# The last stage of an attention and experts kernel: one copy moved, a chunk's end split, doubled expert weights, the last chunk's end in halves

## What is computed

```python
    x = L0_attn_x
    x = x + _layernorm(_L0_attn_ref(_layernorm(x, axis=-1), ...), axis=-1)
    x = x + _layernorm(_L0_ffn_ref(_layernorm(x, axis=-1), ...), axis=-1)
...
        scores0 = x[:, 0, :] @ Wr + br
        _, idx = jax.lax.top_k(scores0, k)
        W1g, b1g = (W1[idx], b1[idx])
        W2g, b2g = (W2[idx], b2[idx])
        h = jnp.einsum('bsd,bkde->bkse', x, W1g) + b1g[:, :, None, :]
        h = jax.nn.gelu(h, approximate=False)
        o = jnp.einsum('bkse,bkef->bksf', h, W2g) + b2g[:, :, None, :]
        return jnp.sum(o, axis=1) / k
```

## Time and profile before

| | us |
|---|---|
| median of 3 runs (2047.66 to 2054.5) | 2049.87 |
| the profiled execution's own time | 2049.51 |
| its span, first to last instruction | 2047.8 |
| PE, DVE, ACT, POOL busy in the span | 1976.5, 1791.3, 1363.0, 305.4 |
| last stage, from its first matrix product at 1690.6 | 357.2 |

### The profile page before, as it was taken

How to read it: one execution, slowest core, us unless ns; L and a number is a source line. 1 busy time by engine, 2 the same in 40 slices (tenths; PEclk the granted TensorE clock), 3 DMA queues, 4 the chain that set the end, 5 groups by cost and what they waited for, 6 DMA issues and landing times.

```text
span 2047.8 us, 39736 instructions
## 1 busy us (share of the span) xinstructions
PE 1976.5 (97%) x15772; PEld 869.5 (42%) x15772; DVE 1791.3 (87%) x3564; ACT 1363.0 (67%) x1653; POOL 305.4 (15%) x373
## 2 busy tenths in 40 slices
PE   9999999999999999999999999999999996999996
PEld 6655333333333333333333333333333324667664
DVE  6876999999999999989999999999899917898883
ACT  5766757777777777777777777777777781333332
POOL 4333101011010101011010101111010104322000
PEclk9999999999999999999999999999999997999999
DMA  5877515050322304041423505051332034454320
GB/s 171 259 230 202 111 37 101 7 92 22 79 50 49 74 23 91 8 90 27 77 45 51 91 8 90 7 92 34 67 58 41 17 109 113 116 138 112 91 67 31
DMA packets 144907, 162.44 MB, mean 79 GB/s; under 512 B 52946, under 2 KB 118610, under 8 KB 144722
## 3 DMA queue, kind: packets, MB, share of 16 engines
q1 hardware_dynamic: 137554, 147.26, 31.2%
q0 software_dynamic: 7168, 12.64, 2.8%
HBM read 99.77 MB, written 59.77 MB: 78 GB/s over the span
## 4 chain that ended last, share of the span: by engine, by line
PE 81%; DVE 11%; ACT 4%; issue 2%; DMA 1%; SPq 1%; POOL 0%; ACTq 0%; POOLq 0%; DVEq 0%
PE b_psO L1121 25%; PE b_psS L1104 25%; PE b_ring L615 13%; PE a_psQK L906 6%; DVE b_pmax L631 4%; PE c_psH L1501 3%; PE a_psV L918 3%; PE c_psO L1514 3%; ACT b_prob L1068 2%; PE b_ring L613 1%; PE c_psA L1471 1%; DVE c_ln_x_stats L81 1%; DVE c_attn L105 1%; DVE c_ln_f_stats L81 1%; PE a_psT L881 1%
## 5 line engine op out<-in xcount | busy, mean ns | idle before, releaser
L631 DVE TENSOR_REDUCE b_pmax<-b_ring 128x1 f32<-128x512 f32 (+4 forms) x2284 | 1336.7, 648 | 75.1 <-PE b_ring L615 59.2
L1068 ACT ACTIVATE b_prob<-b_psS 128x1024 f32<-128x1024 f32 (+3 forms) x1280 | 1085.2, 895 | 367.3 <-PE b_psS L1104 362.6
L1104 PE MATMUL b_psS<-g_qT,g_kT 64*128 64x512 bf16 (+6 forms) x5120 | 833.2, 347 | 10.1 <-ACT b_prob L1068 7.2
L615 PE MATMUL b_ring<-g_kT,g_qT 64*128 64x512 bf16 (+2 forms) x2500 | 714.5, 348 | 2.9 <-DVE b_pmax L631 1.5
L1121 PE MATMUL b_psO<-b_prob,g_v 128*32 128x512 f32 (+3 forms) x5120 | 595.0, 540 | 0.3
L1104 PEld LDWEIGHTS b_psS<-g_qT,g_kT 64*128 64x128 bf16 (+1 forms) x5120 | 295.4, 94 | 460.6 <-ACT b_prob L1068 343.4
L1039 POOL TENSOR_SCALAR_AFFINE_SELECT b_prob<-b_prob 128x512 f32<-128x512 f32 x256 | 162.7, 636 | 1315.8 <-ACT b_prob L1068 1315.5
L615 PEld LDWEIGHTS b_ring<-g_kT,g_qT 64*128 64x128 bf16 x2500 | 221.2, 94 | 234.2 <-DVE b_pmax L631 162.4
L613 PE MATMUL b_ring<-later,query_of 64*128 64x128 bf16 x988 | 191.9, 219 | 3.0 <-DVE b_pmax L631 2.4
L1121 PEld LDWEIGHTS b_psO<-b_prob,g_v 128*32 128x32 f32 x5120 | 103.4, 108 | 172.1 <-issue 131.9
L1501 PE MATMUL c_psH<-c_yT,c_w1e 128*128 128x512 f32 x256 | 119.4, 613 | 22.0 <-ACT c_hT L1426 21.7
(11 more groups left out here) (119 smaller groups left out, 1060.5 us busy)
## 6 DMA issues: line engine op xcount, KB each, us to landing
qk_parts<-a_parts SPq DMA_DIRECT2D x64, 384.0 KB, 4.5
g_qT<-qk_parts SPq DMA_DIRECT2D x184, 128.0 KB, 3.9
g_kT<-qk_parts SPq DMA_DIRECT2D x184, 128.0 KB, 5.1
out_sums<-b_outT SPq DMA_DIRECT2D x64, 256.0 KB, 2.4
v_ones<-a_v SPq DMA_DIRECT2D x16, 544.0 KB, 5.8
g_v<-v_ones SPq DMA_DIRECT2D x32, 272.0 KB, 5.3
a_x<-in_L_attn_x SPq DMA_DIRECT2D x16, 512.0 KB, 5.2
c_x<-in_L_attn_x SPq DMA_DIRECT2D x16, 512.0 KB, 7.3
```

The lines of the kernel that those rows point to most:

```text
L615: ins_ = self.nc.tensor.matmul(to, groups.qT[own, g, h // 2, 0, t * P:(t + 1) * P], groups.kT[own, g, h // 2, 0, pc * CH:pc * CH + w], sta ...
L631: self.nc.vector.tensor_reduce(pmax[:, c % 2].rearrange("p (h t) n -> p h t n", t=TT)[:, heads[0]:heads[-1] + 1:2, qt, pc], bank[:, 0:k * ...
L1068: nc.scalar.activation(prob[:, j % PBUF, 2 * s:2 * s + 2, off:CH], psS[:, 2 * s:2 * s + 2, off:CH], ACT.Exp).then_inc(exp_done, 1)
L1104: ins_ = nc.tensor.matmul(psS[:, 2 * s + p, off:CH], kT[own, g, s, ab, kt * P:(kt + 1) * P], qT[own, g, s, ab, c * CH + off:(c + 1) * CH], ...
```

## The change

Four edits, all in `stage_c` (and the number of tiles becomes a parameter of `LayerNorm`).

1. ACT's order: copy_y(n+2) comes ahead of root_ffn(n). From step 13 on the order is another one: step 13 is gelu(13), copy_y(15), gelu(14), root_ffn(13); step 14 is gelu(15), root_ffn(14); step 15 is root_ffn(15).
2. DVE's order: `experts_end` is cut after the variance. The rest (normalise, add, release the store) is a new function `experts_out`, and take_projection(n+4) stands between the two.
3. Two sets of expert weights and biases, chosen by the parity of the sequence. SP's two waits ahead of overwriting now look one sequence further back and fall away for the first two sequences.
4. The last chunk's end is done in two halves of two tiles, each with its own small layer norm (`ln_last`): `outer` raises `o_done` after tile 1 and after tile 3, DVE takes half 0 through to its output and then half 1, and SP stores each half with its own DMA.

In the diff stand, in this order, the waits of `load_experts` and the last stores on SP, the cut of `experts_end` with the two new functions on DVE, DVE's order and ACT's order:

```diff
-                if not (isinstance(b, int) and b == 0):
-                    sp.wait_ge(gelu_done, b * NC * 2 * KD + 2)
+                if b > 1:
+                    sp.wait_ge(gelu_done, (b - 1) * NC * 2 * KD + 2)
...
-                sp.wait_ge(o_read, b * NC + 1)
+                if b > 1:
+                    sp.wait_ge(o_read, (b - 1) * NC + 1)
...
+                        for h, t in enumerate(HALVES):
+                            sp.wait_ge(out_done, n + 1 + h)
+                            sp.dma_start(out_t[n, :, t], out_sb[:, c % 2, t]).then_inc(stored[c % 2], 16)
...
                 ln_f.variance(chain, ffn, var_f)
+            def experts_out(b, c, n):
+
+                p = c % 2
+                chain = Chain(v, chain_f, n * LN_MARKS + LN_MARKS - 1)
                 v.wait_ge(std_f, n + 1)
                 ln_f.normalise(chain, ffn, ffn).then_inc(norm_f, 1)
                 v.wait_ge(norm_f, n + 1)

                 v.wait_ge(stored[p], 16 + (b * 2 + c // 2) * 16)
                 nc.vector.tensor_tensor(out_sb[:, p], x1[:, c], ffn[:, :, :], ALU.add).then_inc(out_done, 1)
+
+            def last_end():
+
+                v.wait_ge(out_done, LAST)
+                v.wait_ge(stored[LAST % 2], 16 + (B * NC // 2 - 1) * 16)
+                for h, t in enumerate(HALVES):
+                    ln, chain = ln_last[h], Chain(v, chain_l[h], 0)
+                    v.wait_ge(o_done, LAST + 1 + h)
+                    chain.mark(nc.vector.scalar_tensor_tensor(
+                        out=ffn[:, t], in0=psO[:, t], scalar=0.5,
+                        in1=b2mean[:, :].unsqueeze(1).to_broadcast([P, TT // 2, D]), op0=ALU.mult, op1=ALU.add))
+                    chain.wait()
+                    ln.variance(chain, ffn[:, t], var_f)
+                    v.wait_ge(std_f, LAST + 1 + h)
+                    chain.mark(ln.normalise(chain, ffn[:, t], ffn[:, t]))
+                    chain.wait()
+                    nc.vector.tensor_tensor(out_sb[:, LAST % 2, t], x1[:, NC - 1, t], ffn[:, t], ALU.add
+                                            ).then_inc(out_done, 1)
...
                 for k, part in ((2, normalise_x1), (1, route), (3, add_attention), (0, experts_end),
-                                (4, take_projection), (2, route)):
+                                (4, take_projection), (0, experts_out), (2, route)):
...
-                order = ((0, gelu), (3, root_attn), (3, root_x1), (0, root_ffn), (2, copy_y))
+                n = b * NC + c
+                order = ((0, gelu), (3, root_attn), (3, root_x1), (2, copy_y), (0, root_ffn))
+                if n >= UNLED - 1:
+                    order = ((0, gelu),) * (n < UNLED) + ((2, copy_y), (1, gelu), (0, root_ffn))
```

More of the change, by code:

```diff
@@ L103, in normalise @@
         chain.wait()
-        for t in range(TT):
+        for t in range(self.tiles):
             last = v.tensor_scalar(dst[:, t], src[:, t], self.mean[:, t:t + 1], self.rstd[:, t:t + 1],
@@ L1188, in stage_c @@
         ln_f = LayerNorm(nc, sb, "c_ln_f")
+        ln_last = [LayerNorm(nc, sb, f"c_ln_l{h}", tiles=TT // 2) for h in range(2)]
         psT = pb("c_psT", [P, KD, CH], F32)
@@ L1222, in stage_c @@
         stored = [sem(f"c_stored{p}") for p in range(2)]
+        chain_l = [sem(f"c_chain_l{h}") for h in range(2)]
+        LAST = B * NC - 1
+        UNLED = LAST - 1
+        HALVES = [slice(0, TT // 2), slice(TT // 2, TT)]
         W_LOADS = 4
@@ L1289, in _ @@
             for p in range(2):
-                sp.wait_ge(stored[p], 16 + 16 * B * NC // 2)
+                sp.wait_ge(stored[p], 16 + 16 * (B * NC // 2 + p))
         @block.gpsimd
@@ L1402, in step @@
                             route(to_route(b, c))
+                    elif which and part in (experts_end, experts_out) and which[2] == LAST:
+                        if part is experts_end:
+                            last_end()
                     elif which:
```

64 lines of the change are left out of this document (35 added, 29 removed).

## The result

| | before | changed |
|---|---|---|
| median of four runs, us | 2052.18 (2047.66 to 2055.05) | 2034.54 (2033.25 to 2038.79) |
| the profiled execution, and its span | 2049.51, 2047.8 | 2038.79, 2037.1 |

What follows compares the result with a forecast made beforehand. PE was taken to set the pace, so its waits can be won: 2.7 (step 1) + 6.8 (middle) + 2.7 (step 13) + 2.84 + 2.81 + 0.7 = 18.55 us, from 2049.87 to 2031.4 us; range 2026.5 to 2036.5 (0.89).

Steps and rivals of the forecast that it cites:

- The tail on ACT: Steps 14 and 15: GELUs ahead of roots and table loads remove stalls of 2.57 and 2.55, gaining 2.84 and 2.81 us.
- the last end in halves: End of the last step: the split gives 0.4 us on DVE and the smaller second store 0.3 us.
- The middle steps: Nine steps from hidden(3): 5.1 us of smaller stalls, 0.5 of restarts, 1.2 of weight waits, 6.8 us in all.
- It shows only where DVE runs late, and I count it as 0: Split of the chunk's end: DVE's gain per step, some tenths of a us from a shorter root wait, counted as 0.
- DVE can follow at 18.1: Middle: steps 2, 5, 10 and 11 had no stall at 0.4 us lag, so DVE keeps up with 18.1 us steps.
- Two sets of experts: Outer in two steps: w2's DMAs go out some 2 us earlier, so the whole 1.2 us wait for weights goes.
- Step 1: Stall shrinks from 3.77 to 2.76 us and the eight products behind it take 3.7 us; 2.7 us gained.
- Step 13: Stall shrinks from 3.74 to 2.73 us and the products behind it run at the higher clock; 2.7 us gained.
- the lower clock stays: Rival, steps 1 and 13: one or both stalls of 2.75 us still cost 1.7; 2033.1 or 2034.8 us, chance 0.16.
- I take 0, since 2.75 is 0.2 from the stalls without it and 1.0 from those with it: Steps 1 and 13: clock loss behind each shortened stall, bounded by 0 and 1.7 us, is taken as 0.
- the signs of being wrong: Products of 5.4 us behind 2.75 stalls; POOL's product beside normalise_x1 and again the projection's; DVE waiting for `psO` at the end.
- the slower rival: Middle: POOL's product holds DVE twice a step, each stall 2.9 us, 21.3 us a step; 2052 us, chance 0.03.

Runs made afterwards that it cites:

- e5: Changed kernel with the last chunk's end in one piece (one layer norm, one store); median 2035.5 us.
- e4: Changed kernel with ACT's order in the tail as in all other steps (copy ahead of the root, then the GELUs); median 2036.5 us.
- e2: Changed kernel with the chunk's end undivided, experts_out ahead of take_projection; median 2040.02 us.
- e8: Changed kernel with POOL's product cut to 2 of 1024 columns from chunk 4 on, so results are wrong; 2031.0 us in a single run.
- e11: Changed kernel with POOL's product moved to DVE from chunk 4 on, two chunks earlier than needed, ahead of the attention's sum; median 2030.78 us.
- e1: Changed kernel with the copy behind the root again in all steps but the tail's; median 2038.06 us.
- e6: Kernel before with only the copy moved ahead of the root in every step; ratio 0.9993 (0.9972 to 1.0013) to the kernel before, median 2049.3 us.
- e3: Changed kernel with one set of experts' weights and SP's waits as before; median 2036.2 us.
- e7: Changed kernel with the average of the experts' last biases done ahead of the attention's sum on DVE; median 2032.5 us.
- e13: e11 with the tail's order one step earlier and without ACT's own wait for expert weights; median 2027.88 us, ratio 0.9879 to the kernel before.

## Why the prediction was right, and where it was not

- **The tail on ACT and the last end in halves** (2.84, 2.81 and 0.7 us): right in size and mechanism. Step 14 and the last stretch came out at 13.77 and 23.51 us as summed, and DVE's half 1 followed half 0 with no wait for PE. e5 bears out the 0.7; e4 shows both stalls come back (1.68 and 2.55 us).
- **The middle steps** (6.8 us): the sum was right (6.2 and 7.3 us in two profiles), its parts were not. The step that failed is "It shows only where DVE runs late, and I count it as 0" with "DVE can follow at 18.1": the split is worth 2 to 5 us beside the copy (e2), and DVE did not follow at 18.1 everywhere, since stalls of 0.5 to 0.9 us stayed in steps 4, 5, 8 and 9. Without POOL's product the middle is 165.4 us instead of 167.8 to 170.8 (e8, e11). The forecast knew of the hold of 1.0 to 2.2 us and left it in; what it took as fixed was how late the variance comes, so that each stall would shrink by the whole of the copy. The copy is worth at most 3 us beside the split (e1), and nothing measurable alone (e6). That the parts need each other is shown; that an earlier GELU speeds PE up until DVE and the weights have to follow is my reading of it, and e6 can't tell these two apart. The sum came out partly by luck: the copy gave less than its 5.6 and the split more than its 0.
- **Two sets of experts** (1.2 us): right mechanism, mis-sized. The two waits of `outer` in steps 4 and 8 are gone as forecast, but with one set they would have been 2.7 us at the new order (e3); what was read from before was their size at the old one. The forecast that all waits for weights go to 0 failed: hidden(4) waits 0.46 us and outer(0) 0.82.
- **Step 1** (2.7 us, with the high clock): the forecast stall was 2.76. The two profiles have 0.65 and 3.06, the latter with the lower clock. The forecast size describes neither, because it held fixed what varies: whether POOL's product meets DVE's normalisation in step 0 (below).
- **Step 13** (2.7 us, 1.7 of it the clock): the stall shrank to 2.84, forecast 2.73, and the clock fell in the first profile (the rival "the lower clock stays", once) and not in the second. The step that failed is "I take 0, since 2.75 is 0.2 from the stalls without it and 1.0 from those with it": it assumed that the length decides. Of the signs of being wrong this one came true (5.40 us behind 2.84), and another by half: in steps 1, 4, 5 and 8 POOL's product ran beside normalise_x1 (3.41 to 3.53 us instead of 1.38), where the forecast had it meet the projection's normalisation as before, but never beside both in one step, as the slower rival needed.
- **The remainder**, 298.1 against a forecast 297.5 us, is the sum of a missed 1.7 in step 13, 0.6 in the middle, 0.1 in the stall of step 13 and a step 1 that was 2.1 better than forecast, with step 0 0.3 longer. The profile agreed with the forecast partly by luck, and so did its total.

## What to carry to other kernels

Before crediting a stall to the last instruction in front of it, look at the busy time of each engine in single steps: an engine busy for 18.3 of 18.9 us is the first suspect, whatever the wait names, and a run without a part of its work tests it (e8). Here moving its work about within the step gained nothing in the middle (e7), and taking the hold off it did (e11). An elementwise instruction "given away" to POOL can cost DVE more than doing it itself: here about 1.9 us against 1.2. But a wait that stood on POOL then stands on DVE: count the stretch in which the data aren't there yet too. And where nothing on PE's path needs a root, put the GELUs ahead of it, and keep a second wait off the first instruction behind a table load.

## What the runs showed of the hardware

**Between 2.0 and 2.9 us the length of an idle time did not decide the clock.** The eight products behind a stall take 3.70 us at the higher of the two levels. After the same 2.84 or 2.85 us in step 13 they took 5.40 in three profiles (changed, e2, e11), 5.09 in e6, and 3.70 in three more with stalls of that length (e3, e4, e5; e8 the same after 2.83) and in the second profile of the changed kernel. Two rows of that one:

```profile
1761.09 5.40 PE L1545 MATMUL c_psH<-c_yT,c_w1e 128*128 128x512 f32 x8 [3.06 <-ACT c_hT L1462]
...
1985.24 3.70 PE L1545 MATMUL c_psH<-c_yT,c_w1e 128*128 128x512 f32 x8 [2.85 <-ACT c_hT L1462]
```

After 1.96 us ahead of `outer` it fell (e6), and after 2.22 in the same place of step 8 it did not (7.17 us, e6). After 2.09 us it fell (e7), after 2.55 it did in e4 (5.25 us) and did not in the kernel before. After 2.94 and more it fell each time: behind six stalls for a GELU, e1's 5.26 us behind 3.14 among them, and behind e8's wait of 7.38 us for weights. So between 2.0 and 2.9 us either can come, in one kernel too (2.84 and 2.85 in the changed one, so the order of its instructions does not decide it either). What else decides wasn't settled; a row of set idle times would be the run for it.

**POOL's product holds single small instructions of DVE until it ends**, not only the wide ones of the earlier trace rows. In step 0 of the changed kernel a 128x4 instruction that takes 0.17 us alone (first row DVE, second POOL):

```profile
1757.94 2.16 DVE L84 TENSOR_TENSOR c_ln_f_tmp<-c_ln_f_stats 128x4 f32<-128x4 f32 x1
...
1757.74 2.34 POOL L1321 TENSOR_TENSOR c_cc<-c_cc,c_inv 128x1024 f32<-128x1024 f32 x1 [5.39 <-DMA c_inv<-inverse_sums]
```

(The Trainium skill, "SBUF — State Buffer", section "SBUF: two separate sides", tells of such a lock between the two engines, in which the later one waits for the whole instruction; by these rows and e8 the trace agrees.)

**The stall of step 1 goes with what POOL's product meets in step 0.** Where hidden(0) waited 0.88 us or more for the experts' weights (changed, e2, e3, e4, e5), step 1 stalled 0.20 to 0.74 us; where it waited 0.31 or less (before, e1, e6, e7, the second profile of the changed kernel), 1.41 to 3.77 us. DVE's rows of step 0 divide the profiles in the same way: the normalisation of a projection took 1.38 to 1.66 us in the first group and 2.69 to 3.50 in the second, where the product ran beside it. Of the changed kernel, first profile and second:

```profile
1749.38 1.65 DVE L105 TENSOR_SCALAR c_attn<-c_attn,c_ln_a_mean,c_ln_a_rstd 128x256 f32<-128x256 f32 x4
```

```profile
1745.94 3.02 DVE L105 TENSOR_SCALAR c_attn<-c_attn,c_ln_a_mean,c_ln_a_rstd 128x256 f32<-128x256 f32 x4
```

These 1.37 us are over half of the 2.4 by which the two stalls differ. The rest is that DVE began this piece 1.0 us later after hidden(0); my reading, which no run tests by itself, is that a longer wait of hidden(0) lets DVE catch up. e7 shows the worst: the product of one chunk ran beside the normalisation (3.50 us instead of 1.38), and that of the next held a small instruction of the chunk's end for 2.35 us. In e11 to e13, where POOL makes no product there, step 1 took 18.1 us each time, after waits of 0 to 0.7 us.
